# A decoder layer on one core: a new order of the attention loop on four engines, and other banks

## What is computed

```python
x = x + self_attention(layernorm(x))           # 16 query heads of 16, 4 key groups, rope, window 64, 4 sinks
x = x + cross_attention(layernorm(x), ctx)     # 16 heads, causal, no projections: softmax(q k^T / 4) v
x = x + shared_ffn(layernorm(x)) + top4_of_16_experts(layernorm(x))
```

## Time and profile before

| what | us |
|---|---|
| median of 3 runs | 381.97 |
| the runs | 377.18 to 382.44 |
| profiled execution: its own time | 379.63 |
| its span, first to last instruction | 377.8 |
| loop, iterations 0 to 7 | 17.09 to 168.10 |
| tail up to the first expert blocks | 168.10 to about 236.5 |
| expert blocks and end | about 236.5 to 377.8 |

### The profile page before, as it was taken

How to read it: one execution, slowest core, us unless ns; L and a number is a source line. 1 busy time by engine, 2 the same in 40 slices (tenths; PEclk the granted TensorE clock), 3 DMA queues, 4 the chain that set the end, 5 groups by cost and what they waited for, 6 DMA issues and landing times.

```text
span 377.8 us, 8178 instructions
## 1 busy us (share of the span) xinstructions
PE 321.8 (85%) x2388; PEld 246.7 (65%) x2388; DVE 244.2 (65%) x733; ACT 186.2 (49%) x537; POOL 146.1 (39%) x179
## 2 busy tenths in 40 slices
PE   8967778788888897757789996999999999999954
PEld 3434455555555674535667865888888888888743
DVE  2166648686868658853567777766667667664685
ACT  1164468685858656661855742444444444442210
POOL 2741303434334324266716781234344344344000
PEclk9999899999999989985689998999999999999995
DMA  6993292595969683311201233477778777773841
GB/s 212 319 418 144 62 299 63 155 262 174 246 180 238 192 213 112 104 48 45 102 31 44 104 123 106 140 228 226 229 213 237 228 222 231 226 216 124 328 174 56
DMA packets 44183, 66.81 MB, mean 177 GB/s; under 512 B 5379, under 2 KB 32020, under 8 KB 43636
## 3 DMA queue, kind: packets, MB, share of 16 engines
q1 hardware_dynamic: 39508, 54.91, 49.6%
q0 software_dynamic: 3792, 10.56, 7.5%
q10 hardware_dynamic: 848, 0.92, 0.7%
HBM read 37.07 MB, written 29.30 MB: 176 GB/s over the span
## 4 chain that ended last, share of the span: by engine, by line
PE 34%; issue 21%; ACT 16%; DVE 13%; POOL 12%; DMA 3%; POOLq 0%; DVEq 0%; ACTq 0%; SPq 0%
POOL y_picks L595 12%; ACT probs L631 11%; PE bank L1409 9%; PE bank L1334 6%; PE bank L1326 5%; PE bank L1322 4%; PE bank L1368 2%; PE bank L1382 2%; DVE neg_max L868 2%; PE bank L1534 2%; DVE w_l L1139 1%; DVE hid_l L1118 1%; PE bank L1360 1%; DVE yg L1249 1%; ACT values_t L644 1%
## 5 line engine op out<-in xcount | busy, mean ns | idle before, releaser
L631 ACT ACTIVATE probs<-bank,neg_max 128x128 f32<-128x128 f32 x256 | 70.7, 398 | 24.0 <-DVE neg_max L868 24.0
L595 POOL DMA_INDIRECT y_picks<-yb,ids x47 | 45.1, 959 | 74.5 <-DVE yb L1216 73.9
L868 DVE TENSOR_REDUCE neg_max<-bank 128x4 f32<-128x512 f32 x64 | 41.5, 684 | 19.1 <-PE bank L1326 19.1
L1674 PE MATMUL bank<-w,hbt 128*128 128x256 f32 x188 | 48.2, 380 | 0.0
L1334 PE MATMUL bank<-ident,probs 128*128 128x128 f32 x256 | 41.4, 291 | 6.0 <-ACT probs L631 6.0
L1334 PEld LDWEIGHTS bank<-ident,probs 128*128 128x128 f32 x256 | 30.0, 147 | 19.8 <-ACT probs L631 16.1
L532 POOL DMA_INDIRECT x_slots<-x,slots x32 | 33.9, 1059 | 22.2 <-DVE slots L986 13.9
L504 POOL TENSOR_TENSOR rstd<-ve,expo 128x1 f32<-128x1 f32 x16 | 9.2, 574 | 65.8 <-DVE ve L909 65.6
L778 ACT ACTIVATE xbt_h<-bank 128x256 fp32r<-128x256 f32 x47 | 18.0, 384 | 32.8 <-PE bank L1644 32.6
L1674 PEld LDWEIGHTS bank<-w,hbt 128*128 128x128 f32 x188 | 32.1, 190 | 2.5
L1209 DVE TENSOR_TENSOR hb<-sg,bank 128x176 f32<-128x176 f32 x47 | 15.9, 338 | 24.5 <-ACT sg L786 24.5
(11 more groups left out here) (173 smaller groups left out, 692.1 us busy)
## 6 DMA issues: line engine op xcount, KB each, us to landing
x_slots<-zero_b SPq DMA_DIRECT2D x16, 1072.0 KB, 10.8
w<-w_in_dram SPq DMA_DIRECT2D x47, 256.0 KB, 3.2
xb<-x_slots SPq DMA_DIRECT2D x47, 134.0 KB, 2.9
w<-w_in_dram SPq DMA_DIRECT2D x4, 1408.0 KB, 12.0
yg<-y_picks SPq DMA_DIRECT2D x8, 512.0 KB, 8.0
sw_raw<-shared_in_dram SPq DMA_DIRECT2D x6, 384.0 KB, 3.4
ktc<-keys_in_dram SPq DMA_DIRECT2D x8, 256.0 KB, 3.0
ctx_sb<-ctx_in_dram SPq DMA_DIRECT2D x1, 1024.0 KB, 13.1
```

The lines of the kernel that those rows point to most:

```text
L595: pool.indirect_dma_start(y_picks[:, :], bass.IndirectOffsetOnAxis(ids[:, n:n + 1], 0), yb[:, n % RB, :], None).then_inc(yb_placed[n % RB] ...
L631: ins = act.activation(probs[:, g, j, :], ps_s[kind][g][:, 128 * j:128 * j + 128], ACT.Exp, bias=neg_max[:, kind, g, j:j + 1])
L868: dve.tensor_reduce(neg_max[:, kind, g, :], ps_s[kind][g].rearrange("p (j n) -> p j n", j=BLK), AX.X, ALU.max, negate=True).then_inc(max_r ...
L1674: ins = pe.matmul(ps_yb[n % 2][:, 0:D], hbt[:, n % 2, k, :], w2[:, n % RB, k, :], start=k == 0, stop=k == KC - 1)
```

## The change

No operation of the computation is added or dropped. What changes is where each stands in its engine's queue, three banks, and which engine makes some of the copies.

- The projection part of self-attention (turn_attn, take_attn_t, project, the addition, statistics and second_norm) moves from the end of iteration t into iteration t+1, between the self scores and the transposes. cross_queries and cross scores of t-1 follow the front_c of t+1.
- The third norm of tile t-2 becomes that of t-3. Transposes of the cross probabilities' group 3 move to the next iteration.
- front_a(t+2) moves up: on TensorE behind the transposes of self group 3, on ScalarE ahead of exps(CROSS, t-1, 0). front_n(t+2) on VectorE stays behind the four cross maxima.
- ScalarE copies self group 2 and cross group 1; VectorE the other six (before: four and four).
- Attention transposes, the projection and cross queries use bank 4 (ps_x) in place of 6 and 7. Logits and ranks of the first lot move from bank 4 to 7, and from iteration 6 to iteration 7 and the tail.
- POOL: turn(t+1) is first; inverse_deviation(SELF, t-1) follows it (before, it ended the iteration before). The first scatters start in the tail, after the loop's last pieces.
- The loop proper is t = 3 to 5; 0, 1, 2, 6 and 7 are written out.
- Several waits go, since the new order or bank implies them; two come in (ScalarE before exps(SELF, t, 3), TensorE in scores for group 3).

In the diff, the removed lines of the functions printed above are left out.

```diff
...
@@ -532,52 +532,54 @@
                     pool.indirect_dma_start(x_slots[:, :], bass.IndirectOffsetOnAxis(slots[:, TOPK * b + k:TOPK * b + k + 1], 0),
                                             x[:, b, :], None).then_inc(scattered, 16)
...
+            def iteration(t):
+                when = t if isinstance(t, int) else 3
+                if when < B - 1:
+                    turn(t + 1)
+                if when < 2:
                     pool.wait_ge(var1_ready, 2 + t)
                     pool.tensor_tensor(rstd1[:, LATER[t]], ve1[:, LATER[t]], expo[:, LATER[t]], ALU.pow
                                        ).then_inc(rstd1_ready, 1)
...
+                if when >= 1:
+                    inverse_deviation(SELF, t - 1)
+                if when >= 3:
+                    keep_rows(t - 3)
+                if when >= 2:
+                    split_shared(t - 2)
+                if when >= 1:
                     pad_context(t - 1)
...
+                if when >= 2:
+                    inverse_deviation(CROSS, t - 2)
+            iteration(0)
+            iteration(1)
+            iteration(2)
+            pool.wait_ge(rstd1_ready, 3)
+            with pool.Fori(3, B - 2) as t:
+                iteration(t)
+            iteration(B - 2)
+            iteration(B - 1)
+            inverse_deviation(SELF, B - 1)
+            keep_rows(B - 3)
+            pad_context(B - 1)
+            inverse_deviation(CROSS, B - 2)
             pool.wait_ge(rows_zeroed, 16 * (NE + 1))
             pool.wait_ge(gate_loaded, 96)
             pool.wait_ge(xn3_kept, LOT)
             pool.wait_ge(slots_ready, 1)
             scatter(0, 0, 2)
...
+            keep_rows(B - 2)
+            scatter(0, 2, 4)
             scatter(1, 0, 2)
...
+            inverse_deviation(CROSS, B - 1)
             scatter(1, 2, 3)
...
+            keep_rows(B - 1)
             scatter(1, 3, 4)
             scatter(2)
             scatter(3)
             pool.wait_ge(xn3_kept, B - 1)
             pool.wait_ge(slots_ready, 2)
...
+            scatter(4)
             scatter(5)
             scatter(6)
             pool.wait_ge(xn3_kept, B)
...
@@ -663,48 +665,48 @@
                 act.activation(ex[:, bs, :], ex[:, bs, :], ACT.Exp).then_inc(exps_ready, 1)
                 act.activation(ex_g[:, bs], logits_of(i)[:, :, NE], ACT.Exp, scale=-1.0).then_inc(exps_ready, 1)
...
+            def iteration(t):
+                when = t if isinstance(t, int) else 3
+                if when >= 1:
+                    take_attn_t(t - 1)
                 for g in range(3):
                     exps(SELF, t, g)
...
+                if when >= 2:
+                    act.wait_ge(probs_t_psum[CROSS], 4 * (t - 2) + 4)
+                exps(SELF, t, 3)
+                take_probs_t(SELF, t, 2)
+                if when < B - 1:
+                    front_c(t + 1)
+                if when >= 1:
+                    cross_q(t - 1)
+                if when < B - 2:
+                    front_a(t + 2)
+                if when == B - 1:
+                    route_exps(0)
+                if when >= 1:
+                    exps(CROSS, t - 1, 0)
+                if when >= 2:
                     take_values(CROSS, t - 2)
...
+                if when >= 3:
+                    take_xth(t - 3, ps_x)
+                if when >= 1:
                     exps(CROSS, t - 1, 1)
+                    exps(CROSS, t - 1, 2)
+                    take_probs_t(CROSS, t - 1, 1)
                 take_values(SELF, t)
...
+                if when >= 1:
                     exps(CROSS, t - 1, 3)
...
             front_a(0)
             front_c(0)
             front_a(1)
...
+            iteration(0)
+            iteration(1)
+            iteration(2)
+            with act.Fori(3, B - 2) as t:
+                iteration(t)
+            iteration(B - 2)
+            iteration(B - 1)
             def gate(n):
...
@@ -987,62 +991,64 @@
                                          top_f[:, bs, 0:TOPK], float(REGION), slot_s[:, bs, :], ALU.mult, ALU.add
                                          ).then_inc(slots_ready, 1)
...
+            def add_rows(t):
                 dve.wait_ge(wo_psum, t + 1)
                 if isinstance(t, int):
                     dve.wait_ge(xb_ready, 1)
...
+                dve.tensor_tensor(one(x2, t), ps_x[:, 0:D], one(x2, t), ALU.add).then_inc(x2_ready, 1)
+            def iteration(t):
+                when = t if isinstance(t, int) else 3
+                row_max(SELF, t, 0)
+                row_max(SELF, t, 1)
+                if when >= 3:
+                    third_norm(t - 3)
+                if when < B - 1:
+                    front_r(t + 1)
+                row_max(SELF, t, 2)
+                row_max(SELF, t, 3)
+                if when >= 1:
+                    add_rows(t - 1)
+                    statistics(SELF, t - 1)
+                if when < 2:
+                    dve.wait_ge(x_rest, 16)
+                    first_norms(LATER[t])
+                if when == B - 1:
+                    route_shift(0)
+                take_probs_t(SELF, t, 0)
+                if when < B - 1:
+                    front_p(t + 1)
+                if when >= 1:
+                    second_norm(t - 1)
+                take_probs_t(SELF, t, 1)
+                if when >= 2:
+                    take_probs_t(CROSS, t - 2, 3)
+                if when >= 1:
+                    row_max(CROSS, t - 1, 0)
+                    row_max(CROSS, t - 1, 1)
+                take_probs_t(SELF, t, 3)
+                if when >= 1:
+                    row_max(CROSS, t - 1, 2)
+                    row_max(CROSS, t - 1, 3)
+                if when == 0 or when == 1:
+                    dve.wait_ge(rstd1_ready, 2 + t)
+                if when < B - 2:
+                    front_n(t + 2)
+                if when >= 2:
+                    cross_rows(t - 2)
+                if when >= 3:
+                    take_xtl(t - 3, ps_x)
+                if when >= 1:
+                    take_probs_t(CROSS, t - 1, 0)
+                if when >= 2:
+                    statistics(CROSS, t - 2)
+                if when >= 1:
+                    take_probs_t(CROSS, t - 1, 2)
+                normalise(SELF, t, inv, attn)
+                if when < B - 1:
+                    front_v(t + 1)
...
@@ -1139,22 +1145,30 @@
                 dve.tensor_tensor(w13_l[:, e, :, :], w13[:, e, :, :], w13_h[:, e, :, :].bitcast(F32), ALU.subtract
                                   ).then_inc(w13_low, 1)
+            route_top(0)
+            route_pick(0)
+            third_norm(B - 3)
+            take_probs_t(CROSS, B - 2, 3)
+            add_rows(B - 1)
+            statistics(SELF, B - 1)
+            route_slots(0)
             second_norm(B - 1)
             cross_rows(B - 2)
             statistics(CROSS, B - 2)
...
             row_max(CROSS, B - 1, 0)
             row_max(CROSS, B - 1, 1)
...
+            take_xtl(B - 3, ps_x)
+            third_norm(B - 2)
             row_max(CROSS, B - 1, 2)
             row_max(CROSS, B - 1, 3)
+            take_probs_t(CROSS, B - 1, 0)
+            take_xtl(B - 2, ps_x)
+            take_probs_t(CROSS, B - 1, 3)
             low_expert(0)
             low_expert(1)
             route_shift(1)
             for e in range(2, 6):
                 low_expert(e)
...
@@ -1297,8 +1311,6 @@
             def front_c(f):
                 pe.wait_ge(qk_ready, f + 1)
-                if not isinstance(f, int) or f >= 2:
-                    pe.wait_ge(qtc_ready, f - 1)
                 for u in range(2):
                     pe.transpose(ps_w[:, 128 * u:128 * u + 128], qk[:, 128 * u:128 * u + 128], ident[:, :])
                 pe.wait_ge(k_padded, f + 1)
@@ -1315,7 +1327,9 @@
                 else:
                     queries, keys = qtc[:, :, :], [ktc[:, u, :, :] for u in range(2)]
                 for g in range(TILES):
-                    if g < TILES - 1 and kind == CROSS:
+                    if g == TILES - 1 and kind == CROSS and (not isinstance(b, int) or b):
+                        pe.wait_ge(probs_t_ready[CROSS][g], b)
+                    elif g < TILES - 1 and kind == CROSS:
                         pe.wait_ge(probs_t_ready[SELF][g], min(b + 2, B) if isinstance(b, int) else b + 2)
                     elif g < TILES - 1 and (not isinstance(b, int) or b >= 2):
                         pe.wait_ge(probs_t_ready[CROSS][g], b - 1)
@@ -1337,8 +1351,6 @@
             def self_values(b):
                 pe.wait_ge(v_ready, b + 1)
-                if isinstance(b, int) and b == 1:
-                    pe.wait_ge(x2_ready, 1)
                 for g in range(TILES):
                     pe.wait_ge(probs_t_ready[SELF][g], b + 1)
                 for g in range(TILES):
@@ -1352,7 +1364,6 @@
                 for g in range(TILES):
                     pe.wait_ge(probs_t_ready[CROSS][g], c + 1)
                 pe.wait_ge(c_pad_ready, c + 1)
```

(48 more changed lines are left out.)

200 lines of the change are left out of this document (25 added, 175 removed).

## The result

| | before | after |
|---|---|---|
| median of the runs, us | 382.08 | 430.51 |
| lowest and highest, us | 377.18, 382.44 | 426.10, 432.97 |
| profiled execution, us | 379.63 | 430.58 |
| its span, us | 377.8 | 428.7 |
| mean granted TensorE clock | 0.948 | 0.900 |

The changed kernel takes 1.126 times as long (95% interval 1.112 to 1.140). The forecast was 398 us, with a range of 387 to 412: the direction was right and the size was not. The span grew by 50.9 us where the sum of the prediction had 19.

A forecast was written before the change was run, and what follows sets the result against it. No engine is full in the loop; a circle of waits between TensorE, VectorE and ScalarE sets the round. 379.63 + 13 (iterations) - 2 (tail) = 390.6, + 8 (clock) = 398.6, stated as 398 us, range 387 to 412.

The forecast's parts named there:

- The round: Loop, t = 3 to 5: one round takes 22.5 instead of 18.5 us, 4.0 more in each.
- the step that costs most: ScalarE's front_a copy waits for front_n behind four cross maxima: 3.5 us lost on ScalarE, TensorE waits 3.1 us.
- signs of being right: scores(SELF) 22.5 us apart, scores(CROSS) about 9 in, ScalarE idle 6, TensorE idle 3, t = 6 shorter, 0.50 clock behind that hole.
- signs of being wrong: A round under 20 us, front_a without a wait, or a tail over 34 us to the second lot's slots.
- Other iterations: t = 0: 12.0 against 15.06; t = 1: 22.8 against 21.2; t = 2: 22.3; t = 6: 19.1; t = 7: 20.3 us.
- the walk: Instruction-by-instruction timing of one iteration, t = 3 to 5, from the first self mask: cross scores at 9.15, next zero at 22.5.
- The clock: Loop, t = 1 to 5: clock falls in three or four rounds at 2 to 2.5 us, +8 us, bounds 0 and +25.
- Rival 2: Loop: the clock is lost in nearly every round and stays down, 410 to 416 us; chance 0.09.
- the rule of the Trainium skill: TensorE's throttled clock is the default, sustained activity releases it; alone, five loop rounds at 2 to 5 us, 10 to 25.
- The tail: After the loop: added work and later scatters, their delay taken by 13.9 us of slot waiting; -2 us, bounds -5 and +2.
- Edits priced at nothing: Two copies moved to VectorE, the other bank and the DMAs' places: zero; the copies at most 1.2 us a round.
- Blocks and end: Expert blocks and end of the kernel after the tail: same work as before, 0 us.

The follow-up runs named there:

- the filler: The changed kernel with 13 extra matmuls of 128x512 zeros, results unused, ahead of TensorE's front_a in t = 1 to 5: 422.75 us, ratio 1.116.

## Why the prediction was right in direction and wrong in size

**The round.** Right. The step from cross masks to front_n, front_a, the exponentials and VectorE's copy of C2 stands in the trace in that order, and the round was 23.2 instead of the forecast 22.5. The 0.7 is spread: 0.3 up to the cross masks, 0.15 up to front_a, 0.05 at the exponentials and 0.2 behind. The experiment with front_n moved shows the step that costs most: without it the round is 20.1. There I was wrong in a smaller way, since the prediction gave 19.1 for a round without front_a. All its signs of being right came (the 22.5 as 23.2 where the clock held), and so did one of its signs of being wrong: the tail took 36.6 us, over 34, to the second lot's slots.

**Other iterations.** t = 0 was 13.0 (12.0 forecast), t = 6 19.55 (19.1), t = 7 22.0 (20.3). In t = 1, 28.6 instead of 22.8, a mechanism was missed. The cross masks came 12.65 us into it, 3.5 later than the walk's 9.15 for a full round, of which the prediction had some 2 for the first_norms on VectorE. A second POOL instruction, the root for four tiles, stands ahead of second_norm's root:

```profile
39.49 1.02 POOL L541 TENSOR_TENSOR rstd<-ve,expo 128x4 f32<-128x4 f32 x1 [1.43 <-DVE ve L838]
40.48 0.55 POOL L504 TENSOR_TENSOR rstd<-ve,expo 128x1 f32<-128x1 f32 x1
...
41.06 0.46 DVE L929 TENSOR_SCALAR xn<-x,mv,rstd 128x256 f32<-128x256 f32 x1 [0.93 <-POOL rstd L504]
...
42.54 1.87 PE L1336 MATMUL bank<-masks,ident_b 128*128 128x512 bf16 x4 [0.52 <-issue]
...
189.16 1.86 PE L1336 MATMUL bank<-masks,ident_b 128*128 128x512 bf16 x4 [0.52 <-issue]
```

I had priced those first_norms on VectorE alone, and not in POOL's queue ahead of inverse_deviation(SELF, 0). VectorE stood 0.93 us for it. The row at 189.16 shows that t = 7 also did its cross scores at the low clock.

**The clock.** Mechanism right, size too small. Forecast: three or four of five rounds at 2 to 2.5 us, 8 in all. Measured: t = 2, 3 and 5 lie 3.2, 2.8 and 1.6 above the clean t = 4, and t = 0 lies 1.05 above the 11.98 that the kernel with front_n moved took at 1.00. That is 8.7. t = 1 is 5.8 above its forecast, of which 0.9 is POOL's root, so up to 4.9 more are the clock; t = 7 has part of its 1.7. The loop's clock term was thus some 9 to 15. That t = 2 and 3 are the clock's work is shown by the filler; the shares in t = 0, 1, 5 and 7 rest on comparison of lengths alone. The prediction also read the masks as 1.87 us instead of 0.86; the 0.86 leaves out what overlapped the group before, and the like length at full clock is 1.02, as at 120.31. Rival 2 asked for nearly every round and a clock that stays down: four of five rounds with the hole were hit, but t = 4 had a hole of 2.88 us and kept 1.00. By the rule of the Trainium skill (TensorE: Matmul & The Clock Gate, Part 1) as the prediction read it, five rounds at 2 to 5 us, 10 to 25; the trace lands at its low end.

**The tail.** This is the step that failed. "POOL's 32 scatters [...] now they start 8 to 9 us into the tail, with this waiting time to take the delay", -2 with bounds -5 and +2. Measured: +4.8 up to the slots and +12.4 behind them. The first scatter did start 11 us in. But the prediction let the old waiting time of 13.9 us absorb a delay as if POOL's queue could be filled in any order. The diff puts inverse_deviation(CROSS, 7), which needs the statistics of the last tile, ahead of scatters that need nothing new; everything behind it waits. At front_a the prediction did ask what is queued behind a wait ("cross_values, third_norm and turn_values"); at this line of the diff I didn't ask it. 12.2 us of the 17.2 are this, as the two experiments with POOL's order show in both directions. The other 4.8 us stay open. The clock was 0.51 from 216 to 233 us,

```profile
216.00:233.00 17.00, 13.06 (x73) 11.14 (x74) 8.12 (x14) 9.43 (x23) 4.26 (x5) 0.51 0.09 34
```

but over the whole stretch from the end of t = 7 to the slots its mean was 0.72, against 0.68 before, so some 20 us were spent at the low clock in both. A lower clock does not explain it. The tail's added work may: TensorE was busy 27.8 us in that stretch instead of 25.0, VectorE 22.7 instead of 17.1. No run tests it.

**Edits priced at nothing.** Blocks and end: +1.3. VectorE's load in t = 4 is 14.38 us of 23.19, near the 14.5 of the prediction, which leaves room for the two copies. Neither they nor the new banks were tested alone, so that they cost and gain nothing is not shown.

**Summed up.** Of the 32 us between forecast and profiled execution, the tail has 19.2 (12.2 POOL's queue), the loop 11.6 (clock up to 7, POOL's root in t = 1 0.9, the rest the round's 0.7 and like amounts), and the blocks 1.3. With the scatters' queue counted the same sum would have been near 411.

## What to carry to other kernels

When an order is changed, write down for each in-order queue what stands behind every waiting instruction, the DMA-issuing instructions above all: a wait for a late tile's 128x1 root held ten ready scatters and cost 12 us. Where a copy is needed by another engine, its place ahead of independent work on its own engine is worth measuring alone: front_n moved ahead of four row maxima gave 26 us back, and one copy moved ahead in the old kernel gave a kernel faster than either order. A hole on TensorE that is on the path cost its own length here (2.9 us, and 3.1 a round were won by closing it) and up to some 3 us more a round when the clock fell in it; price both, and try zero matmuls in the hole to tell them apart.
